# Whitening of two chunks in seven as four 64x64 matmuls at a time, in a float32 whitening, AFNO and MLP kernel

## The chip, the cores and the metric

The kernel runs on one core of one Trainium2 chip. The metric is the device time of one execution in microseconds; lower is better. Engines are named as the profile names them: PE is TensorE (PEld its weight loads), DVE VectorE, ACT ScalarE, POOL GpSimd, SP SyncE.

## The reference

The input is a float32 batch of 16 images of 56x56 pixels with 64 channels. Two layers follow each other.

1. **Whitening.** Over all 50,176 pixels the mean and the 64x64 covariance are taken; with L the Cholesky factor of the covariance (with a little of the unit matrix added), each pixel becomes inverse(L) @ (x - mean), times gamma, plus beta.
2. **An AFNO block.** Layer norm; a real 2D FFT of each image; a small two-layer complex MLP on the spectrum (block diagonal, 8 blocks of 8 channels; relu, then soft shrinkage by 0.01); the inverse FFT, plus its input, plus the residual; a second layer norm; an MLP 64 to 256 to 64 with gelu; plus the residual.

```
f_hat = solve_triangular(cholesky(cov), eye) @ (x - mean);  x1 = f_hat * gamma + beta
h  = afno_filter(layer_norm(x1)) + x1          # rfft2, block MLP, irfft2, + its input
out = gelu(layer_norm(h) @ mw1 + mb1) @ mw2 + mb2 + h
```

## The kernel before

**Tiling.** The 16 images are worked on in 8 pairs. A pair is a tile of 112 partitions (2 images x 56 rows) by 3584 columns (56 pixels x 64 channels), held as 28 blocks of 128 columns; a block has an even pixel column in its first 64 channels and an odd one in its last 64. After a first phase (covariance, elimination, the whitening matrix) the main loop `step(i)`, i = 0 to 7, does the spectral part of pair i, the whitening and first layer norm of pair i+1, the second layer norm and the MLP of pair i-1, and the transposes of pair i+2.

**Whitening.** `transpose_x` (L855) turns the pair's blocks so that the 128 (pixel, channel) rows lie on partitions; ACT copies them to `xT` (L1093). `whiten(i, ks)` (L871) then does chunks of four blocks, seven chunks per pair: for a block, the stationary operand is `xT`'s 128x112 piece, the moving operand is `wy`, 128x128. `wy` holds the 64x64 whitening matrix twice, on its diagonal, and zeros elsewhere. A chunk fills one PSUM bank (112x512). DVE adds beta and writes it to `ybuf` (`ev_whiten`, L623). Pairs from 1 on use bank 0 for chunks 0 to 4 and banks 1 and 2 for chunks 5 and 6. A float32 matmul shows in the trace as two passes, each with a weight load, so a chunk of four matmuls is eight records.

**Order.** Every engine's program is written out by hand, and engines wait for each other by semaphores. In `step(i)` PE does `dft_h(i)` (L887, eight chunks; behind its chunks 2 and 4 come `mlp_out` L982 and `turn_out` L991 of pair i-2's last slice), whitening chunk 0 of pair i+1, `dft_w(i)` (L897), chunk 1, `layer_1(i)` (L910), chunk 2, `transpose_n(i-1, 0)` (L964), chunk 3, and then slices in which the MLP (L973, L982) is mixed with chunks 4 to 6, `layer_2` (L926), `inv_w` (L937) and `inv_h` (L950).

Waits that matter here: `dft_w` begins when ACT has copied all of `dft_h` (L1101). `layer_1` writes the banks of eight chunks; DVE evicts the odd ones, each in two operations (`ev_layer_1`, L632), and ACT the even ones (L1136). `transpose_n(i-1, 0)` begins when all eight are evicted. Chunk k+1 in bank 0 waits until DVE has evicted chunk k, so chunk 3 waits for DVE's eviction of chunk 2.

DVE's program in `step(i)` for i > 1: one eighth of the statistics of pair i-1 (L539), the output add of pair i-2's last slice (`ev_mlp`, L658, waits for L991), the rest of the statistics, `ln2(i-1)` (a chain of small operations, L559 to L415, then the eviction of whitening chunk 0, then two multiplications L582), the eviction of chunk 1, `ev_layer_1(i)`, and the eviction of chunk 2.

**Banks.** Bank 3 (`BANK_M`) belongs to the MLP's transposes and outputs (L964, L982, L991). `c_dve` counts DVE's output adds, seven per pair; `a_dve` counts evicted whitening chunks, seven per pair; `pe_a` counts chunks of transposes and of whitening that PE has finished.

The tile modes of PE that occur: whole array (L855, L871, L887, L897, L937, L964, L991), two parts of 64 rows (L910, L950, L973; L950 has 58 rows and puts the two in banks of their own), and two parts of 64 columns (L926, L982).

Of the kernel before, what the change touches and what calls it, by code (L numbers as in the profile page):

```python
# [25 lines left out]
ALU = mybir.AluOpType  # L26
# [3 lines left out]
B, H, W, C = 16, 56, 56, 64  # L30
# [6 lines left out]
ROWS = 2 * H  # L37
# [16 lines left out]
BANK_X, BANK_M, BANK_HID = 0, 3, 4  # L54
# [31 lines left out]
def before_in_bank(banks):  # L86

    last = {b: k for k, b in enumerate(banks)}
    out = []
    for k, b in enumerate(banks):  # L90
        out.append((last[b], k <= last[b] and b not in banks[:k]))
        last[b] = k
    return out


B_BANK = [(1, 2, 4, 5, 6, 7)[k % 6] if k < L2 else 1 + k % 2 for k in range(B_CHUNKS)]
FIRST_WHITEN = (0, 1, 2, 3, 0, 1, 2)
WHITEN = (BANK_X,) * 5 + (1, 2)
B_BEFORE = before_in_bank(B_BANK)

# [16 lines left out]
C_ACT, C_DVE = len(C_ACT_DONE), SLICES  # L117
# [21 lines left out]
def build(nc, x, consts, params, out):  # L139
# [5 lines left out]
    with ExitStack() as ctx:  # L145
        def sb(name, shape, dtype=F32):
            return ctx.enter_context(nc.sbuf_tensor(name, shape, dtype))

        def sem(name):
            return ctx.enter_context(nc.semaphore(name))  # L150
# [7 lines left out]
        def pp(name, rows=128):  # L158
            return prm[0:rows, p_at[name][0]:p_at[name][1]]

        ident = cc("ident")
        wy = sb("wy", [128, 128])
# [10 lines left out]
        ybuf = sb("ybuf", [ROWS, FREE])  # L173
# [4 lines left out]
        xT = sb("xT", [128, WP * ROWS])  # L178
# [58 lines left out]
        x_in, pe_a, pe_b, pe_c = sem("x_in"), sem("pe_a"), sem("pe_b"), sem("pe_c")  # L237
        a_act, a_dve = sem("a_act"), sem("a_dve")
        b_act, b_dve = sem("b_act"), sem("b_dve")
        c_act, c_dve = sem("c_act"), sem("c_dve")  # L240
# [9 lines left out]
        bank = [psum[:, j, :] for j in range(8)]  # L250
# [20 lines left out]
        def row(name, n):  # L271

            return pp(name, ROWS).unsqueeze(1).broadcast_to((ROWS, n, C))
# [17 lines left out]
        with nc.Block() as block:  # L291
# [116 lines left out]
            def _(dve):  # L408
# [199 lines left out]
                def ln2(i):  # L608
                    mean_rstd(i, 1)
                    if i < PAIRS - 2:  # L610
                        ev_whiten(i + 2, [0])
                    for k in range(2):
                        multiply_rstd(i, k)

                def ev_whiten(i, ks):
                    if i == 1:
                        dve.wait_ge(r_begun, 1)
                    elif i > 1:

                        dve.wait_ge(r_ready, 2 * i - 1)  # L620
                    for k in ks:
                        dve.wait_ge(pe_a, i * A_CHUNKS + 7 + k + 1)
                        nc.vector.tensor_tensor(  # L623
                            ybuf[:, k * 512:(k + 1) * 512].rearrange("p (w c) -> p w c", c=C),
                            bank[(WHITEN if i > 0 else FIRST_WHITEN)[k]][0:ROWS, :].rearrange("p (w c) -> p w c", c=C),
                            row("beta", 8), ALU.add).then_inc(a_dve, 1)
# [54 lines left out]
                def step(i, ahead, behind):  # L681
# [13 lines left out]
                    if behind:  # L695
# [3 lines left out]
                        for k in range(5, 8):  # L699
                            ln2_stats(i - 1, k)  # L700
                        ln2(i - 1)
                    next_(ev_whiten, [1] if behind else [0, 1])
                    ev_layer_1(i)
                    slice_(0, lambda: next_(ev_whiten, [2, 3, 4]), lambda: next_(ev_whiten, [5]),
                           lambda: next_(ev_whiten, [6]), lambda: next_(ln1_stats, [0]))
                    slice_(1, lambda: ev_layer_2(i, [0]), lambda: (ev_layer_2(i, [1]), next_(ln1_stats, [1])),
# [51 lines left out]
            def _(pe):  # L758
# [100 lines left out]
                def whiten(i, ks):  # L859

                    pe.wait_ge(a_act, i * 7 + 7)
                    for k in ks:
                        if i == 0:
                            if k >= 4:
                                pe.wait_ge(a_dve, k - 3)
                        elif 0 < k < 5:
                            pe.wait_ge(a_dve, i * 7 + k)
                        t = bank[(WHITEN if i > 0 else FIRST_WHITEN)[k]]
                        for j in range(4):
                            w = 4 * k + j  # L870
                            last = nc.tensor.matmul(t[0:ROWS, j * 128:(j + 1) * 128], xT[:, w * ROWS:(w + 1) * ROWS],  # L871
                                                    wy[:], start=True, stop=True)
                        last.then_inc(pe_a, 1)
# [135 lines left out]
                def step(i, ahead, ahead2, behind):  # L1009
# [8 lines left out]
                    def whiten_next(j):  # L1018
                        if ahead and j < 3:
                            whiten(i + 1, [4 + j])  # L1020
# [9 lines left out]
                    if ahead:  # L1030
                        whiten(i + 1, [0])
                    dft_w(i)
                    if ahead:
                        whiten(i + 1, [1])
# [326 lines left out]
```

## Time and profile before

| | |
|---|---|
| median of 3 runs | 880.11 us (878.37 to 880.96) |
| profiled execution, its own time | 884.47 us |
| its span, first to last instruction | 882.7 us |
| PE busy | 790.9 us (90%) |
| DVE busy | 577.6 us (65%) |
| ACT busy | 367.1 us (42%) |
| POOL busy | 250.6 us (28%) |
| mean granted TensorE clock | 0.92 of full speed |

A row of the profile names the line, the engine, the operation, what it writes and reads, the shape and the count; times are in microseconds from the start of the span. The PE records of one line that follow each other are merged into one piece with a count of passes. The end of a matmul record is modelled and includes its way through the array, so the time that a group takes from its neighbours is read from start to start. "[0.41 <-X]" is idle time before an instruction and what ended it, as far as the profile can tell; where an instruction waits for several semaphores the name can be the wrong one.

### The profile page before, as it was taken

Reading aid. Unit: us, or ns where it says so; the run is one execution under the profiler, and the core shown is the slowest. Engines: PE = TensorE matmul, PEld = TensorE weight load, DVE = VectorE, ACT = ScalarE, POOL = GpSimd, SP = SyncE. Lnnn points to the kernel's source line nnn. Section 1 sums busy time; section 2 is a strip of 40 time slices with the busy share of each in tenths; the row PEclk is TensorE's granted clock in tenths of the full one; section 3 lists DMA queues with packets and bytes.
Section 4 is the critical chain, followed back from the end, with each engine's and each line's share of the span. In section 5 each row is a group of like instructions: output and inputs, shape, how many; then the busy total and the mean of one; then the engine's idle time right before and its main releaser. Section 6 shows DMA issues by size and latency. Waiting matters only on the chain.

```text
span 882.7 us, 16525 instructions
## 1 busy us (share of the span) xinstructions
PE 790.9 (90%) x6585; PEld 558.3 (63%) x6585; DVE 577.6 (65%) x1868; ACT 367.1 (42%) x660; POOL 250.6 (28%) x106
## 2 busy tenths in 40 slices
PE   5898997598599999999999999999999999899576
PEld 5895655477286658675766767586657755575232
DVE  4465677639666858585876768586858686652621
ACT  0001100263046645564556455545645453555244
POOL 4000000274531271218142604541271228040000
PEclk9996556599789999999999999999999999999889
DMA  9970200200200112011200300130100011001001
GB/s 267 269 184 1 74 0 1 74 0 18 59 1 1 33 32 85 12 33 36 70 23 22 104 2 23 32 95 2 32 27 17 12 33 32 1 22 32 22 28 46
DMA packets 9964, 40.98 MB, mean 46 GB/s; under 512 B 1232, under 2 KB 1232, under 8 KB 8208
## 3 DMA queue, kind: packets, MB, share of 16 engines
q1 hardware_dynamic: 9888, 39.92, 16.1%
q8 instruction: 53, 0.87, 0.4%
q14 instruction: 23, 0.19, 0.1%
HBM read 27.07 MB, written 12.85 MB: 45 GB/s over the span
## 4 chain that ended last, share of the span: by engine, by line
PE 76%; DVE 16%; DMA 4%; issue 3%; ACT 2%; DVEq 0%; ACTq 0%
PE psum L973 11%; PE psum L982 10%; PE psum L887 7%; PE psum L950 6%; PE psum L897 6%; PE psum L926 6%; PE psum L937 6%; PE psum L910 5%; PE psum L871 5%; DMA xin<-x_dram 4%; PE psum L807 3%; PE psum L771 3%; PE psum L855 3%; DVE stats L539 3%; PE psum L991 3%
## 5 line engine op out<-in xcount | busy, mean ns | idle before, releaser
L1156 ACT ACTIVATE hid<-psum,hbias 128x448 f32<-128x448 f32 x224 | 124.1, 635 | 90.7 <-PE psum L973 90.7
L394 POOL TENSOR_TENSOR p_y<-layer,clamped 128x512 f32<-128x512 f32 x64 | 75.4, 1178 | 240.9 <-DVE clamped L649 240.9
L973 PE MATMUL psum<-n2T,mw1s 64*128 64x448 f32 x448 | 104.2, 585 | 3.4 <-ACT n2T L1149 3.4
L982 PE MATMUL psum<-hid,prm 128*64 128x448 f32 x448 | 97.2, 555 | 4.0 <-DVE oslice L658 4.0
L1093 ACT ACTIVATE xT<-psum,negm 128x448 f32<-128x448 f32 x56 | 35.6, 636 | 106.5 <-PE psum L855 106.4
L359 POOL TENSOR_TENSOR hbuf<-hbuf,prm 112x3584 f32<-112x3584 f32 x7 | 43.4, 6200 | 111.0 <-DVE hbuf L604 111.0
L950 PE MATMUL psum<-u_r,cst 58*112 58x448 f32 x256 | 60.4, 592 | 15.5 <-DVE rbuf L671 11.3
L623 DVE TENSOR_TENSOR ybuf<-psum,prm 112x512 f32<-112x512 f32 x56 | 38.6, 689 | 50.7 <-PE psum L871 50.3
L926 PEld LDWEIGHTS psum<-w2s,o_g 128*64 128x64 f32 x1856 | 60.1, 138 | 15.5 <-issue 8.9
L937 PEld LDWEIGHTS psum<-cst,p_y 128*128 128x128 f32 x512 | 61.2, 192 | 11.2 <-issue 5.6
L926 PE MATMUL psum<-w2s,o_g 128*64 128x64 f32 x1856 | 66.3, 224 | 2.1 <-DVE layer L643 2.1
L937 PE MATMUL psum<-cst,p_y 128*128 128x112 f32 x512 | 66.7, 277 | 1.2 <-DVE layer L643 1.2
L982 PEld LDWEIGHTS psum<-hid,prm 128*64 128x64 f32 x448 | 27.4, 137 | 63.7 <-issue 46.7
L643 DVE TENSOR_TENSOR layer<-psum,prm 128x512 f32<-128x512 f32 x64 | 40.4, 631 | 41.5 <-PE psum L926 41.5
L887 PE MATMUL psum<-cst,hbuf 112*112 112x116 f32 x512 | 60.4, 280 | 7.3 <-DVE hbuf L604 5.2
L887 PEld LDWEIGHTS psum<-cst,hbuf 112*112 112x112 f32 x512 | 57.6, 191 | 14.5 <-issue 9.0
L1101 ACT COPY u_r<-psum 112x464 f32<-112x464 f32 x64 | 35.0, 546 | 67.5 <-PE psum L887 67.5
L871 PE MATMUL psum<-wy,xT 128*112 128x128 f32 x448 | 59.5, 282 | 3.8 <-DVE ybuf L623 3.2
L871 PEld LDWEIGHTS psum<-wy,xT 128*112 128x112 f32 x448 | 53.1, 182 | 13.4 <-issue 11.3
L539 DVE BATCH_NORM_STATS2 stats<-ybuf 112x6 f32<-112x64 f32 x448 | 61.2, 209 | 0.5
L973 PEld LDWEIGHTS psum<-n2T,mw1s 64*128 64x128 f32 x448 | 40.5, 193 | 32.1 <-issue 23.8
L897 PE MATMUL psum<-cst,u_r 112*128 112x116 f32 x464 | 53.3, 275 | 0.6 <-ACT u_r L1101 0.6
(116 smaller groups left out, 1310.7 us busy)
## 6 DMA issues: line engine op xcount, KB each, us to landing
xin<-x_dram SPq DMA_DIRECT2D x9, 1568.0 KB, 8.6
out_dram<-oslice SPq DMA_DIRECT2D x56, 224.0 KB, 2.2
ybuf<-x_dram SPq DMA_DIRECT2D x2, 1568.0 KB, 19.3
fbuf<-x_dram SPq DMA_DIRECT2D x2, 1568.0 KB, 22.4
n<-x_dram SPq DMA_DIRECT2D x2, 1568.0 KB, 25.2
xin<-x_dram SPq DMA_DIRECT2D x4, 392.0 KB, 5.1
prm<-params_dram SPq DMA_DIRECT2D x1, 742.0 KB, 26.9
cst<-consts_dram SPq DMA_DIRECT2D x1, 604.0 KB, 18.5
```

Source lines behind the costliest of these rows:

```text
L394: nc.gpsimd.tensor_tensor(yk, a, b, ALU.subtract).then_inc(y_ready, 1)
L539: last = nc.vector.bn_stats(stats[:, w, :], src[:, w * C:(w + 1) * C])
L871: last = nc.tensor.matmul(t[0:ROWS, j * 128:(j + 1) * 128], xT[:, w * ROWS:(w + 1) * ROWS], wy[:], start=True, stop=True)
L887: last = nc.tensor.matmul(t[0:ROWS, j * 2 * KR:(j + 1) * 2 * KR], h_w[:, 4 * k + j, :], cc("f1", ROWS), start=True, stop=True)
L897: last = nc.tensor.matmul(t[:, j * 4 * KF:(j + 1) * 4 * KF], u_r[0:ROWS, (4 * k + j) * 128:(4 * k + j + 1) * 128], cc("f2", ROWS), start=T ...
L910: one = nc.tensor.matmul(t[b][:, 0:(z - a) * KF], w1s[C * b:C * b + C, 256 * s + 128 * half:256 * s + 128 * half + 128], p_v[C * b:C * b + ...
L926: last = nc.tensor.matmul(t[C * r:C * r + C, j * C:j * C + C], o_g[:, at:at + C], w2s[:, 128 * half + C * r:128 * half + C * r + C], start ...
L937: last = nc.tensor.matmul(t[:, j * 112:j * 112 + 112], y_v[:, 4 * k + j, :], cc("invw"), start=True, stop=True)
L950: one = nc.tensor.matmul(t[d][0:ROWS, 0:7 * C], cc("invh")[rows, ROWS * m:ROWS * m + ROWS], g[rows], start=(m == 0), stop=(m == 1))
L973: nc.tensor.matmul(t[:, 0:4 * ROWS], mw1s[C * v:C * v + C, HH * m:HH * m + HH], n2T[C * v:C * v + C, :], start=True, stop=True).then_inc(p ...
L982: last = nc.tensor.matmul(t[C * v:C * v + C, 0:4 * ROWS], pp("mw2")[:, C * m:C * m + C], hid[:, s % 2, m, v, :], start=(m == 0), stop=(m = ...
L1156: nc.scalar.activation(hid[:, s % 2, m, v, :], bank[C_BANK[k]][:, 0:4 * ROWS], ACT.Gelu, bias=hbias[:, m:m + 1]).then_inc(c_act, 1)
```

## The change

For pairs 2 to 7, whitening chunks 0 and 1 are computed in another way. A block of 128x112 by 128x128 becomes four matmuls: stationary 64 rows (even or odd pixel) by 64 or 48 columns (the first 64 and the last 48 image rows of the 112), moving the 64x64 whitening matrix alone. Each of the four has its own quarter of the array. Even pixels go to bank 0 and odd ones to bank 3, 64 columns per block in each, so a chunk fills 256 columns of both banks. DVE evicts each bank with an operation of its own, 112x256, and writes 64-column groups of `ybuf` at a stride of 128; `a_dve` is raised by the second one. A chunk is 16 matmuls (32 passes) in place of 4 (8 passes). Since bank 3 is now written by chunk 0, PE waits ahead of it until DVE has done all the output adds of pair i-2 (of the pair being whitened minus 2), from pair 3 on. Chunks 2 to 6, and pairs 0 and 1, stay as they are.

```diff
+QUADS = (0, 1)
@@ ev_whiten (DVE)
                     for k in ks:
                         dve.wait_ge(pe_a, i * A_CHUNKS + 7 + k + 1)
+                        if i > 1 and k in QUADS:
+                            for v in range(2):
+                                last = nc.vector.tensor_tensor(
+                                    ybuf[:, k * 512:(k + 1) * 512].rearrange("p (w v c) -> p v w c", v=2, c=C)[:, v],
+                                    bank[BANK_M * v][0:ROWS, 0:256].rearrange("p (w c) -> p w c", c=C),
+                                    row("beta", 4), ALU.add)
+                            last.then_inc(a_dve, 1)
+                            continue
@@ whiten (PE)
                         t = bank[(WHITEN if i > 0 else FIRST_WHITEN)[k]]
+                        if i > 1 and k in QUADS:
+                            if k == 0 and i > 2:
+                                pe.wait_ge(c_dve, (i - 2) * C_DVE)
+                            for j in range(4):
+                                for p, m in ((0, C), (C, ROWS - C)):
+                                    for v in range(2):
+                                        at = (4 * k + j) * ROWS + p
+                                        last = nc.tensor.matmul(bank[BANK_M * v][p:p + m, j * C:(j + 1) * C],
+                                                                xT[C * v:C * v + C, at:at + m],
+                                                                wy[C * v:C * v + C, C * v:C * v + C], start=True, stop=True)
+                            last.then_inc(pe_a, 1)
+                            continue
                         for j in range(4):
```

## Rows read from the trace of the kernel before

**Rows 1.** The page: busy time of PE and DVE, granted clock in 40 slices
```profile
PE 790.9 (90%) x6585; PEld 558.3 (63%) x6585; DVE 577.6 (65%) x1868; ACT 367.1 (42%) x660; POOL 250.6 (28%) x106
...
PEclk9996556599789999999999999999999999999889
```

**Rows 2.** Busy time by stretch: two periods of the main loop, and inside one
```profile
core 0: us, PE busy (x) PEld busy (x) DVE busy (x) ACT busy (x) POOL busy (x), PEclk, DMA share, GB/s
...
345.47:428.34 82.87, 81.18 (x736) 56.46 (x738) 60.58 (x195) 45.18 (x81) 29.89 (x12) 1.00 0.14 40
428.34:511.20 82.86, 81.16 (x736) 56.44 (x738) 60.59 (x195) 45.19 (x81) 29.88 (x12) 1.00 0.14 40
```

**Rows 3.** The chain of waits, 420 to 437 us: start, us, what
```profile
420.00 0.88 PE psum L871 x8
...
427.37 0.88 PE psum L871 x8
428.25 5.90 PE psum L910 x32
...
434.17 0.63 DVE o_g L632
...
435.50 0.70 DVE ybuf L623
...
436.33 1.10 PE psum L871 x8
```

**Rows 4.** PE in order of time, the two idle places behind layer_1, second period
```profile
352.70 0.57 PE L964 MATMUL psum<-cst,n 112*128 112x112 f32 x4 [0.41 <-ACT o_g L1136]
353.47 1.10 PE L871 MATMUL psum<-wy,xT 128*112 128x128 f32 x8 [0.19 <-DVE ybuf L623]
```

**Rows 5.** DVE in order of time, 416 to 437 us
```profile
416.87 0.69 DVE L658 TENSOR_TENSOR oslice<-psum,fbuf 112x512 f32<-112x512 f32 x1 [2.06 <-PE psum L991]
417.48 2.75 DVE L539 BATCH_NORM_STATS2 stats<-rbuf 112x6 f32<-112x64 f32 x21
...
424.86 0.69 DVE L623 TENSOR_TENSOR ybuf<-psum,prm 112x512 f32<-112x512 f32 x1
425.47 3.95 DVE L582 TENSOR_TENSOR n<-rbuf,small 112x1792 f32<-112x1792 f32 x2
429.34 0.68 DVE L623 TENSOR_TENSOR ybuf<-psum,prm 112x512 f32<-112x512 f32 x1
430.06 5.41 DVE L632 TENSOR_SCALAR o_g<-psum,prm 64x435 f32<-64x435 f32 x8
435.50 0.69 DVE L623 TENSOR_TENSOR ybuf<-psum,prm 112x512 f32<-112x512 f32 x1
```

**Rows 6.** DVE in order of time, the same place in step(1)
```profile
264.25 5.48 DVE L632 TENSOR_SCALAR o_g<-psum,prm 64x435 f32<-64x435 f32 x8 [0.94 <-PE psum L910]
```

**Rows 7.** The chain of waits, 358 to 368 us: groups in different tile modes
```profile
358.20 0.39 PE psum L964 x4
...
364.28 1.08 PE psum L926 x32
365.37 0.53 PE psum L964 x4
...
367.95 0.73 PE psum L926 x20
```

**Rows 8.** All engines in order of time, around whitening chunk 0
```profile
420.04 0.55 ACT L1101 COPY u_r<-psum 112x464 f32<-112x464 f32 x1 [0.25 <-PE psum L887]
...
420.64 0.30 PEld L897 LDWEIGHTS psum<-cst,u_r 112*128 112x128 f32 x2
420.72 0.29 PE L897 MATMUL psum<-cst,u_r 112*128 112x116 f32 x1
```

**Rows 9.** DVE evictions by shape: count, busy us, mean ns of one
```profile
L643 DVE TENSOR_TENSOR layer<-psum,prm 128x512 f32<-128x512 f32 x48 | 32.7, 681 | 41.5 <-PE psum L926 41.5
...
L643 DVE TENSOR_TENSOR layer<-psum,prm 128x320 f32<-128x320 f32 x16 | 7.7, 480 | 0.0
```

## The prediction

> **What bounds the kernel now.** I read the page first, for the engines' shares and the clock, then the busy time of two whole periods, then the chain of waits through one period, and then each engine in order of time around the two chunks that change.
>
> PE is busy for 790.9 us of the 882.7 us span, DVE for 577.6 us; the granted clock is below full speed only in the first part, which the change doesn't touch [rows 1]. A period of the loop is 82.87 us, PE is busy for 81.2 us of it, and the clock is 1.00 throughout (2.4 GHz) [rows 2]. By these shares PE is the bound, and any PE time saved would be time saved. The chain says otherwise for one place: it runs through chunk 0 (0.88 us), chunk 1 (0.88) and layer_1 (5.90), then leaves PE for DVE at 434.17, goes through DVE's last layer_1 eviction (L632) and its eviction of whitening chunk 2 (L623), and returns to PE with chunk 3 at 436.33 [rows 3]. PE stands still there twice, 0.41 us ahead of L964 and 0.19 us ahead of chunk 3 [rows 4]. The row gives ACT as what ended the first; but DVE's last L632 ends at 430.06 + 5.41 = 435.47, and the same wait asks for it, so DVE is as likely.
>
> How free DVE is to follow PE decides what the change is worth. From 416.87, when L991 releases it, DVE shows no idle time for a PE result until 436.19: an output add, statistics, the small chain, chunk 0's eviction at 424.86, two multiplications, chunk 1's at 429.34, eight layer_1 operations from 430.06, chunk 2's at 435.50 [rows 5]. What starts that run of DVE work, L991 inside dft_h, lies ahead of both changed chunks. So PE and DVE reach 434.17 together: the chain may be drawn through PE, but DVE alone would come to the same moment. In step(1) it isn't so: DVE waited 0.94 us for layer_1 and then took 5.48 us in place of 5.41 [rows 6].
>
> **PE's part.** A whitening pass of 128 columns takes 0.88 / 8 = 110 ns [rows 3], so a 64-column pass alone should take some 55 ns. Where two parts of the array work side by side on 64 columns (L926), 32 passes take 1.08 us and 20 take 0.73 [rows 7]: (1.08 - 0.73) / 12 = 29 ns a pass, or 58 ns for two at once, and 1.08 - 32 x 0.029 = 0.15 us that doesn't depend on the count. The same 0.15 us shows on the other side: a whole-array group of 4 takes 0.53 us between two column-tiled groups and 0.39 us among its own kind [rows 7]. I take 0.15 us as the price of one change of tile mode.
>
> No row shows four parts at once. Bounds: four at a time at the pass's own length, 8 x 55 ns = 0.44 us for the 32 passes; two at a time, 32 x 29 ns = 0.93 us; one at a time, 32 x 55 ns = 1.76 us. I take four at a time, each round a little longer than the 58 ns of two, 0.48 us: L926 shows two parts overlapping nearly fully in columns, and L910 does in rows (32 passes of 435 or 406 columns, at 110 / 128 ns a column, would be some 11.6 us in a line and take 5.90 [rows 3]). The change puts the two row halves in different banks, as L910 does.
>
> Chunk 0 stands between dft_h and dft_w, both whole-array: two mode changes, 0.48 + 0.30 = 0.78 us against 0.88. But dft_w waits for ACT's last copy of dft_h, which ends at 420.04 + 0.55 = 420.59; dft_w's first weight load starts at 420.64, its first pass at 420.72 [rows 8]. The chunk was just long enough to cover ACT, so the 0.10 us is worth nothing: PE waits instead. Chunk 1 stands ahead of layer_1, which changes the mode anyway: one more change, 0.48 + 0.15 = 0.63 us against 0.88. Layer_1 starts and ends 0.25 us earlier. The new wait for `c_dve` costs nothing: the add that it wants is done at 416.87 + 0.69 = 417.56 [rows 5], over 2 us before chunk 0 at 420.00; behind it on PE stands everything else, but it would bind only if DVE came 2.4 us later. The later users of bank 3 already wait for DVE work that stands behind chunk 1's eviction. No DMA is touched or moved.
>
> **DVE's part.** An eviction of 512 columns becomes two of 256. In L643, 192 columns more take 681 - 480 = 201 ns [rows 9], 1.05 ns a column, so 256 columns last about 0.69 - 0.27 = 0.42 us. One operation starts before the last has fully ended: L582 starts 425.47 - 424.86 = 0.61 us after the 0.69 us eviction starts [rows 5], an overlap of 0.08. Two take 2 x (0.42 - 0.08) = 0.68 us where one took 0.61: 0.07 us more. From the statistics the fixed part is a little less: 21 operations of 64 columns in 2.75 us [rows 5] are 0.13 us each, 0.067 of it columns, 0.06 fixed. The bounds are 0.06 and, with no overlap at all, 0.84 - 0.61 = 0.23; I take 0.075 a chunk, 0.15 us a pair. Half the columns in each of two banks saves nothing.
>
> **The sum.** In steps 2 to 6, DVE's run from 416.87 is unbroken, so its last L632 ends 0.15 us later, and L964 and chunk 3 with it. PE's 0.25 us goes into its own wait. From there on PE is the bound again and everything moves by the same amount. That is 5 x 0.15 = +0.75 us. In step(1) DVE follows PE: -0.25 us (it has 0.94 us of idle time to lose, and 5.41 us is still shorter than its present 5.48). Together +0.5 us: span 883.2, that execution's own time 884.97. The profiled execution, 884.47, stands 4.4 us above the median of 880.11, and the change goes onto the median: **880.6 us**. About 0.3% (2.6 us) is what a measurement of this kernel can tell from no change; this forecast is within it.
>
> **Rivals.**
>
> *A. Two at a time.* The 29 ns a pass of L926 may be what the engine can start, not what two parts can do. Each chunk streams 0.93 us: chunk 0 takes 0.93 + 0.30 = 1.23 (+0.35, and ACT no longer covers it), chunk 1 takes 0.93 + 0.15 = 1.08 (+0.20). Layer_1 ends 0.55 us later, DVE follows PE, and its own 0.15 is covered: 6 x 0.55 = +3.3 us, **883.4**. This is the case on the slower side; it decides once a chunk streams for over 0.73 us, since two chunks then cost PE 2 x 0.73 + 0.45 - 1.76 = 0.16 us, more than DVE's 0.15. Between the forecast and this, three quarters of the way at 0.82 us a chunk, PE would lose 2 x 0.82 - 1.31 = 0.33 us a pair, +2.0 us. For it: no row shows passes closer than 29 ns on average. Against: 29 ns is just half of a pass plus a little, as two parts would give, and layer_1 overlaps as fully at some 370 ns for two passes (5.90 / 16), where starting can't be the limit. The Trainium skill, "TensorE: Matmul & The Clock Gate", section "Wait — 56ns, not 53.3ns?", has a floor of its own: matmuls never start less than about 25 ns apart, however short. By that estimate the chunk streams 32 x 25 = 0.80 us, costs PE +0.22 and +0.07, and the whole comes to +1.7 us; no row here is short enough to show it.
>
> *B. One at a time.* If the four parts get in each other's way (two banks and two column halves at once), 1.76 us a chunk: +1.18 and +1.03 us, 6 x 2.2 = +13 us, **893**. Only that nothing of the kind stands in the trace speaks for it.
>
> *C. PE's gain goes through.* If ACT's and DVE's rows hide slack, all of 0.10 + 0.25 us a pair counts: -2.1 us, **878.0**, still within 0.3%. To be faster by more, mode changes would have to be free as well: 12 x 0.40 = -4.8 us. Against both: DVE's unbroken run.
>
> *D. The change does not do what it says*, and the quarters run as whole-array matmuls: 32 passes of 55 ns without mode changes, much as B.
>
> **How the numbers follow.** Forecast (DVE decides, PE's gain lost) 0.55; the case between it and A, +2.0 us, 0.15; A 0.15; B and D 0.06; C 0.09. The range takes in the forecast, C, the case in between and most of A: 878.6 to 883.6. A median of three moves by about 1 us either way. Slower by over 0.3% (above 882.75): B and D, nearly all of A, a little of the case in between, 0.23. Faster (below 877.5): a part of C, 0.04. Within: 0.73.
>
> **What the changed profile would show.** Right: L871 chunks of 32 passes at 0.5 to 0.8 us; dft_w still starting 0.68 us after the last L1101 does, with PE idle ahead of it; two L623 of about 0.42 us per chunk; the idle time ahead of L964 grown from 0.41 to some 0.8 us in steps 2 to 6, with DVE as its end; a period of 83.0 us. Wrong: 32 passes at 1.1 us or more, and DVE waiting ahead of L632 in every step (A, B); a period below 82.87 (C). It would fail altogether if the pieces outside the two chunks changed length.

## The result, and the profile after

The changed kernel was timed three times against the kernel before. The first timing, 20 executions each, gave a median of 881.84 us (877.89 to 887.47) against 878.13 (874.79 to 890.68), ratio 1.0045 with an interval of 1.0026 to 1.0064. The two later ones, among the experiments below, gave 0.9992 (0.9962 to 1.0023) and 0.9967 (0.9941 to 0.9993). The first and the third contradict each other, so the timings as a whole don't show a sign. The traces can be compared more closely: the loop below repeats to 0.03 us between two executions of the kernel before and to 0.10 us between three of the changed kernel.

First the loop as a whole. PE in order of time, the start of each `dft_w`, changed kernel:

```profile
251.45 6.73 PE L918 MATMUL psum<-cst,u_r 112*128 112x116 f32 x58
334.06 6.73 PE L918 MATMUL psum<-cst,u_r 112*128 112x116 f32 x58
417.06 6.73 PE L918 MATMUL psum<-cst,u_r 112*128 112x116 f32 x58
...
583.06 6.73 PE L918 MATMUL psum<-cst,u_r 112*128 112x116 f32 x58
666.44 6.73 PE L918 MATMUL psum<-cst,u_r 112*128 112x116 f32 x58
748.13 6.73 PE L918 MATMUL psum<-cst,u_r 112*128 112x116 f32 x58 [0.64 <-ACT u_r L1122]
```

and the same three ends in the kernel before:

```profile
254.98 6.66 PE L897 MATMUL psum<-cst,u_r 112*128 112x116 f32 x58
337.85 6.66 PE L897 MATMUL psum<-cst,u_r 112*128 112x116 f32 x58
...
750.80 6.73 PE L897 MATMUL psum<-cst,u_r 112*128 112x116 f32 x58 [0.63 <-ACT u_r L1101]
```

The six stretches from dft_w(1) to dft_w(7), each holding one changed chunk 1 and one changed chunk 0, take 748.13 - 251.45 = 496.68 us; before it was 750.80 - 254.98 = 495.82. The change costs **0.86 us** there, 0.10% of the whole. 0.07 us of it is only a matter of where the reading starts: wherever a changed chunk 0 stands ahead of it, `dft_w` lasts 6.73 us in place of 6.66, and so it does in both kernels at dft_w(7), which has no chunk ahead; from the end of dft_w(1) to the end of dft_w(7) the loss is 0.79. Step by step: 82.61 us in step 1 (before 82.87), 83.00 in steps 2 to 4, 83.38 in step 5, 81.69 in the last (before 81.48).

Step 7, which has no whitening, differs too. PE in order of time behind layer_1(7), the kernel before, then the changed kernel:

```profile
764.86 0.58 PE L964 MATMUL psum<-cst,n 112*128 112x112 f32 x4 [1.47 <-ACT o_g L1136]
766.05 3.43 PE L973 MATMUL psum<-n2T,mw1s 64*128 64x448 f32 x8 [0.62 <-ACT n2T L1149]
769.41 0.61 PE L964 MATMUL psum<-cst,n 112*128 112x112 f32 x4
```

```profile
762.19 0.57 PE L985 MATMUL psum<-cst,n 112*128 112x112 f32 x4 [1.47 <-ACT o_g L1157]
763.39 1.84 PE L994 MATMUL psum<-n2T,mw1s 64*128 64x448 f32 x8 [0.62 <-ACT n2T L1170]
765.16 0.60 PE L985 MATMUL psum<-cst,n 112*128 112x112 f32 x4
```

The same eight passes take 3.43 us and 1.84 us: behind the same idle places of 1.47 and 0.62 us the mean granted clock is 0.71 in the kernel before (764.80 to 767.80 us; it fell from 2.4 to 1.2 GHz there) and 1.00 in the changed kernel (762.13 to 765.13). From dft_w(7) to the last pair's transposes (L964, in the changed kernel L985) it is 78.64 us before and 77.36 after, 1.28 less. That outweighs the loss in the loop: from dft_w(1) to that point the kernel before takes 574.5 us (`null` 574.3) and the changed kernel 574.1 (its second and third profile 573.9), and from dft_w(1) to the end of the span 627.7 us against 627.3, 625.8 and 625.7. So the traces show a loop that is longer by 0.8 to 0.9 us, and from dft_w(1) on a kernel that isn't longer. What follows explains the loop; why the clock stays up in step 7 is open.

Where the loop's loss goes: all engines in order of time, step 2 of the changed kernel (POOL, DVE and PE lines; the rows answer to [rows 4, 5, 8]).

```profile
330.28 0.69 DVE L667 TENSOR_TENSOR oslice<-psum,rbuf 112x512 f32<-112x512 f32 x1 [2.07 <-PE psum L1012]
330.89 2.75 DVE L540 BATCH_NORM_STATS2 stats<-fbuf 112x6 f32<-112x64 f32 x21
331.05 4.05 POOL L385 TENSOR_TENSOR rbuf<-hbuf,ybuf 112x1792 f32<-112x1792 f32 x1 [4.20 <-DVE oslice L667]
...
333.35 0.68 PE L885 MATMUL psum<-wy,xT 64*64 64x64 f32 x32
333.46 0.55 ACT L1122 COPY u_r<-psum 112x464 f32<-112x464 f32 x1 [0.25 <-PE psum L908]
333.68 1.54 DVE L560 TENSOR_TENSOR small<-stats 112x56 f32<-112x56 f32 x1
334.05 6.55 PEld L918 LDWEIGHTS psum<-cst,u_r 112*128 112x128 f32 x58 [0.16 <-ACT u_r L1122]
...
338.29 0.76 DVE L626 TENSOR_TENSOR ybuf<-psum,prm 112x256 f32<-112x256 f32 x2
338.96 3.95 DVE L583 TENSOR_TENSOR n<-fbuf,small 112x1792 f32<-112x1792 f32 x2
340.72 0.68 PE L885 MATMUL psum<-wy,xT 64*64 64x64 f32 x32
341.33 5.92 PE L931 MATMUL psum<-p_y,w1s 64*128 64x435 f32 x32
342.82 0.75 DVE L626 TENSOR_TENSOR ybuf<-psum,prm 112x256 f32<-112x256 f32 x2
343.61 5.41 DVE L641 TENSOR_SCALAR o_g<-psum,prm 64x435 f32<-64x435 f32 x8
...
349.12 0.58 PE L985 MATMUL psum<-cst,n 112*128 112x112 f32 x4 [0.81 <-ACT o_g L1157]
```

Chunk 1 takes 341.33 - 340.72 = 0.61 us from start to start against 0.97 in the kernel before by the same reading (427.21 to 428.18). Not all of these 0.36 us are a gain, since some 0.1 us now stands ahead of the chunk: in `pool_chunk1`, where only chunk 1 is changed, it is 7.20 us from the start of dft_w to that of layer_1, before 7.46 (420.72 to 428.18), 0.26 less. Behind chunk 0 the weight load of dft_w waits for ACT. DVE's evictions take 0.67 and 0.79 us to the next instruction, before 0.61 and 0.72. The wait ahead of L985 is 0.81 us, before 0.41; the row names ACT, but DVE's last L641 ends at 343.61 + 5.41 = 349.02, just ahead of it, and `dve_split` below, where only DVE's work is longer, lengthens the same wait. One row stands out: DVE's L560, a small operation of 56 columns, lasts 1.54 us. POOL's L385 ends at 331.05 + 4.05 = 335.10, L560 at 335.22.

### The profile page after: what moved, and what is told of

Read it like the earlier page. It is cut to its first block, busy times and chain, and to the rows that moved or that the text cites. A ratio compares the mean times of both kernels' runs of the same rounds, so it can differ in the third digit from the quotient of the medians.

```text
span 878.7 us, 17118 instructions
## 1 busy us (share of the span) xinstructions
PE 785.2 (89%) x6873; PEld 551.9 (63%) x6873; DVE 578.8 (66%) x1880; ACT 367.1 (42%) x660; POOL 250.9 (29%) x106
## 4 chain that ended last, share of the span: by engine, by line
PE 65%; DVE 25%; DMA 4%; issue 4%; ACT 2%; DVEq 0%; ACTq 0%
PE psum L994 11%; PE psum L1003 10%; PE psum L971 7%; PE psum L947 6%; PE psum L958 6%; PE psum L908 5%; DVE stats L540 4%; DMA xin<-x_dram 4%; PE psum L892 4%; DVE o_g L641 3%; PE psum L816 3%; PE psum L780 3%; PE psum L864 3%; PE psum L1012 3%; PE psum L918 2%
## 5 line engine op out<-in xcount | busy, mean ns | idle before, releaser
L908 PE MATMUL psum<-cst,hbuf 112*112 112x116 f32 x512 | 57.9, 272 | 7.3 <-DVE hbuf L605 5.2
L908 PEld LDWEIGHTS psum<-cst,hbuf 112*112 112x112 f32 x512 | 55.1, 184 | 14.5 <-issue 9.0
L1122 ACT COPY u_r<-psum 112x464 f32<-112x464 f32 x64 | 35.0, 546 | 65.0 <-PE psum L908 65.0
L632 DVE TENSOR_TENSOR ybuf<-psum,prm 112x512 f32<-112x512 f32 x44 | 30.4, 690 | 46.8 <-PE psum L892 46.6
L918 PEld LDWEIGHTS psum<-cst,u_r 112*128 112x128 f32 x464 | 52.4, 192 | 1.8 <-ACT u_r L1122 1.8
L369 POOL TENSOR_TENSOR rbuf<-ybuf,prm 112x3584 f32<-112x3584 f32 x1 | 7.8, 7757 | 158.9 <-DVE hbuf L605 158.9
```

The source lines that it names most:

```text
L908: last = nc.tensor.matmul(t[0:ROWS, j * 2 * KR:(j + 1) * 2 * KR], h_w[:, 4 * k + j, :], cc("f1", ROWS), start=True, stop=True)
L918: last = nc.tensor.matmul(t[:, j * 4 * KF:(j + 1) * 4 * KF], u_r[0:ROWS, (4 * k + j) * 128:(4 * k + j + 1) * 128], cc("f2", ROWS), start=T ...
```

## The experiments

The loop is compared by the same six stretches throughout, dft_w(1) to dft_w(7), in us:

```
kernel        step 1  step 2  step 3  step 4  step 5  step 6    sum
before         82.87   82.87   82.86   82.87   82.87   81.48   495.82
null           82.87   82.87   82.87   82.88   82.87   81.49   495.85
changed        82.61   83.00   83.00   83.00   83.38   81.69   496.68
dve_split      82.87   82.98   83.01   82.99   83.37   81.60   496.82
chunk1         82.60   82.92   82.94   82.90   82.94   81.55   495.85
one_evict      82.61   82.85   82.92   82.84   82.85   81.54   495.61
stats_after    82.61   82.96   83.05   82.97   83.36   81.67   496.62
pool_before    82.87   82.87   82.87   82.86   82.88   81.49   495.84
pool_after     82.61   82.61   82.61   82.61   82.96   81.31   494.71
pool_chunk1    82.61   82.61   82.61   82.61   82.61   81.24   494.29
shift10        82.87   82.87   82.88   82.88   83.22   81.50   496.22
```

**null: the kernel before against itself.** No edit.

> The kernel before against itself. Both theories: ratio 1.000, an interval of some +-0.3%, a period of 82.87 us in its profile. It shows how far two sets of executions of one program stand apart, and whether the first 250 us (where the clock is below full speed) differ from one execution to the next by as much as the 4 us between the two profiles at hand.

Ratio 1.0003 (0.9985 to 1.0022). The loop is the same to 0.03 us, and yet this profile's span is 878.8 us against 882.7. The stretch ahead of the loop differs: PE in order of time, `null` first, then the kernel before.

```profile
241.35 1.76 PE L950 MATMUL psum<-u_r,cst 58*112 58x448 f32 x8 [1.30 <-DVE rbuf L671]
243.88 6.57 PE L887 MATMUL psum<-cst,hbuf 112*112 112x116 f32 x64 [0.77 <-DVE rbuf L671]
```

```profile
240.79 3.33 PE L950 MATMUL psum<-u_r,cst 58*112 58x448 f32 x8 [1.30 <-DVE rbuf L671]
244.89 9.38 PE L887 MATMUL psum<-cst,hbuf 112*112 112x116 f32 x64 [0.77 <-DVE rbuf L671]
```

The busy time by stretch gives a granted clock of 1.00 between 245 and 255 us for `null` and 0.72 for the kernel before: the clock rose from its lower level (1.2 GHz) to the full one (2.4 GHz) after PE's idle places of step 0, in one execution in time for dft_h(1), in the other in the middle of it. From dft_w(0) to dft_w(1) the profiles show three lengths, about 70.4, 71.9 and 74.7 us, in kernels of either kind. That one stretch spreads by over 4 us, five times the loss in the loop; the stretch ahead of it, up to dft_w(0), takes 175.0 to 182.1 us.

**again and again2: the changed kernel, second and third time.** No edit.

> The changed kernel, a second profile. Theory 1 (DVE's two evictions set the loss and the rest is chance): period 83.01 us in every step from 2 on, sum over the loop +0.5 to +1.0 us against the kernel before, ratio 1.0006 to 1.0012 but for chance. Theory 2 (something in the changed kernel adds about 3 us more, such as stalls that come now and then, or a clock that falls more often): periods of 83.3 us or more in several steps, or a lower granted clock in the loop, ratio 1.003 or more again.

> The changed kernel a third time. The first timing gave a ratio of 1.0045 (1.0026 to 1.0064), the second 0.9992 (0.9962 to 1.0023), while the loop, in both profiles, is 0.8 us longer (0.1%). If the loop's 0.8 us is all, the ratio is near 1.001 again and the first timing was chance in the first and last stages; if not, near 1.004.

Ratios 0.9992 and 0.9967, as above; the loops sum to 496.60 and 496.58 us, periods 82.61, 82.98, 83.0, 82.98, 83.35, 81.7. So the loop's 0.8 us is a property of the program, and the first timing's 3.7 us isn't in the loop. Theory 2 in its form of 3 us more in the loop falls; the one stall in step 5 stands. Why three timings of the same two programs disagree beyond their intervals was not found; the stretches whose clock differs from run to run are the candidates, and only the profiled executions show those. Step 7's isn't one of them. Its MLP ran at the lower clock in all five profiles of kernels that evict each chunk whole (`before`, `null`, `pool_before`, `shift10`, `one_evict`) and at full clock in all nine of the others. So it went with the program; but it isn't PE's part of the change (`dve_split` keeps the clock, `one_evict` doesn't) nor the number of DVE instructions (`shift10`), and no run isolates what it is.

**dve_split: only DVE's part of the change.**

```diff
+                        if i > 1 and k < 2:
+                            for v in range(2):
+                                last = nc.vector.tensor_tensor(
+                                    ybuf[:, k * 512:(k + 1) * 512].rearrange("p (w v c) -> p v w c", v=2, c=C)[:, v],
+                                    bank[BANK_X][0:ROWS, :].rearrange("p (w v c) -> p v w c", v=2, c=C)[:, v],
+                                    row("beta", 4), ALU.add)
+                            last.then_inc(a_dve, 1)
+                            continue
```

> The kernel before, PE untouched; only the evictions of whitening chunks 0 and 1 of pairs 2 to 7 are two operations of 256 columns each instead of one of 512. Theory 1: the period goes from 82.87 to 83.0 us in steps 2 to 6 with no change on PE, the idle time ahead of L964 from 0.41 to 0.55, total +0.7 to +0.9 us, ratio 1.001. Theory 2 (PE's quarter matmuls cost the time): period 82.87, ratio 1.000.

The periods are those of the changed kernel in steps 2 to 5, with PE as before. PE in order of time, step 3:

```profile
422.63 5.92 PE L918 MATMUL psum<-p_y,w1s 64*128 64x435 f32 x32
428.48 1.13 PE L879 MATMUL psum<-wy,xT 128*112 128x128 f32 x8
430.16 0.57 PE L972 MATMUL psum<-cst,n 112*128 112x112 f32 x4 [0.55 <-ACT o_g L1144]
```

The wait grew from 0.41 to 0.55 us: DVE's fixed cost alone makes the loss, and from step 2 on the quarter matmuls neither add to it nor take from it. The sum is +1.00 us, more than was expected, by the long step 5. Ratio 0.9991 (0.9963 to 1.002).

**stats_after: DVE relieved of 1.8 us ahead of its chain.** In the changed kernel:

```diff
-                        ln2_stats(i - 1, 4)
+                        for k in (4, 5, 6):
+                            ln2_stats(i - 1, k)
                         if i > 1:
                             ev_mlp(i - 2, SLICES - 1)
-                        for k in range(5, 8):
-                            ln2_stats(i - 1, k)
+                        ln2_stats(i - 1, 7)
```

> The changed kernel, with two of DVE's eighths of the second layer norm's statistics (14 operations, 1.8 us) moved ahead of the output add that waits for L991, into 2.06 us in which DVE stood idle. Theory 1: DVE is now ahead, PE's shorter chunk 1 counts, the period is 82.87 - 0.25 = 82.6 us in every step from 1 on, the idle time ahead of L964 is back at 0.4, total -1.5 us against the kernel before, ratio 0.998. Rival (PE's gain is lost to something else, or the quarter matmuls cost elsewhere): the period stays at 82.87 or more.

Theory 1 failed here: the periods stayed at 83.0 us, and the ratio is 1.0008 (0.998 to 1.0035). POOL and DVE in order of time, step 3:

```profile
417.73 0.98 DVE L540 BATCH_NORM_STATS2 stats<-rbuf 112x6 f32<-112x64 f32 x7
417.89 4.08 POOL L385 TENSOR_TENSOR fbuf<-hbuf,ybuf 112x1792 f32<-112x1792 f32 x1 [4.17 <-DVE oslice L667]
418.74 3.35 DVE L560 TENSOR_TENSOR small<-stats 112x56 f32<-112x56 f32 x1
```

L560 started 1.8 us earlier and lasted 1.8 us longer. It ends at 422.09, POOL's operation at 421.97: the same 0.12 us behind it as in the changed kernel. Elsewhere in these traces the same operation lasts about 0.26 us. DVE's operation waits for POOL's, inside its own record. Both read two SBUF operands. The Trainium skill, "SBUF — State Buffer", section "SBUF: two separate sides", says that VectorE and GpSimd share one pair of SBUF ports as an exclusive lock, held for a whole instruction, and that a VectorE operation with two SBUF inputs takes it against a GpSimd operation that reads SBUF; the trace agrees (statistics, with one input, run beside POOL at their usual pace in the rows above, and so does an output add in the kernel before, a TENSOR_TENSOR with one input in SBUF and one in PSUM: it lasts 0.68 us from 411.45, in the middle of a POOL add of 409.43 to 413.46). The lock itself is on no row; that POOL's end sets DVE's is what the next runs test. Theory 1b: the start of DVE's chain is set by POOL's add, which waits for L667, which waits for L1012 of PE.

**pool_before and pool_after: POOL's add split, so that little of it is left when L667 is done.** In each of the two kernels:

```diff
-                    for k in range(2):
-                        ws = slice(k * WP, (k + 1) * WP)
+                    for lo, hi, s in ((0, 28, 3), (28, 48, 5), (48, 56, 6)):
+                        ws = slice(lo, hi)
                         if i > 1:
-                            pool.wait_ge(c_dve, (i - 2) * C_DVE + out_done(3 + 3 * k))
-                        nc.gpsimd.tensor_tensor(r4[i % 2][:, ws], h_tok[:, ws], y4[:, ws], ALU.add).then_inc(r_ready, 1)
+                            pool.wait_ge(c_dve, (i - 2) * C_DVE + out_done(s))
+                        last = nc.gpsimd.tensor_tensor(r4[i % 2][:, ws], h_tok[:, ws], y4[:, ws], ALU.add)
+                        if s != 5:
+                            last.then_inc(r_ready, 1)
```

> The kernel before; POOL's second residual add is split so that only its last 8 of 28 pixel columns wait for DVE's last output add (L658), 1.15 us of work after it in place of 4.04. In all traces so far DVE's first small operation of the second layer norm ended 0.12 us after this POOL operation did, however early it started (1.54 us long, 3.35 us in stats_after, 0.26 elsewhere). Theory 1b (POOL's add, not DVE's own work, sets when DVE's chain begins): that operation shrinks to 0.27 us, the chain runs 1.27 us earlier, but PE bounds layer_1, so the period stays at 82.8 to 82.87 us. Rival (DVE's own work was the bound): the operation and the period stay as they are.

> The same POOL split in the changed kernel. Theory 1b: DVE is 1.1 us ahead of layer_1, its longer evictions are covered, PE's shorter chunk 1 counts, and the period is 82.6 us in every step from 1 on, total -1.5 us against the kernel before (ratio 0.998). Rival (PE's gain has nowhere to go whatever DVE does): 82.87 or more.

DVE and POOL in order of time in `pool_after`, step 3:

```profile
411.80 2.75 DVE L542 BATCH_NORM_STATS2 stats<-rbuf 112x6 f32<-112x64 f32 x21
411.96 1.29 POOL L385 TENSOR_TENSOR fbuf<-hbuf,ybuf 112x512 f32<-112x512 f32 x1 [1.29 <-DVE oslice L669]
414.59 0.27 DVE L562 TENSOR_TENSOR small<-stats 112x56 f32<-112x56 f32 x1
...
422.46 0.75 DVE L628 TENSOR_TENSOR ybuf<-psum,prm 112x256 f32<-112x256 f32 x2
424.04 5.48 DVE L643 TENSOR_SCALAR o_g<-psum,prm 64x435 f32<-64x435 f32 x8 [0.83 <-PE psum L933]
```

The small operation is back at 0.27 us, DVE waits 0.83 us for layer_1, and the period is 82.61 us: the 0.26 us of chunk 1 now counts in every step. In the kernel before the same edit is worth nothing (495.84): DVE is early there too (0.94 us idle ahead of its layer_1 evictions), but PE arrives when it did. The periods are as expected but for step 5 of `pool_after`, 82.96 us, which makes its sum -1.1 us where -1.5 was expected. Ratios 1.0007 (0.9977 to 1.0036) for `pool_after` and 1.0006 (0.9973 to 1.0039) for `pool_before`: too wide to see 1.1 us.

**chunk1, pool_chunk1 and pool_chunk1b: quarter matmuls for chunk 1 alone.** `QUADS = (1,)`, with the wait for `c_dve` moved to chunk 1; the last two with POOL's add split.

> The changed kernel with quarter matmuls for chunk 1 only, POOL as before. One eviction is split instead of two: DVE, released by POOL's add, ends layer_1's evictions 0.07 us later than in the kernel before, so the period is 82.94 us in steps 2 to 6 and 82.61 in step 1, total +0.1 us. Rival (the loss comes from chunk 0's part on PE): 82.87.

> As pool_after, but only chunk 1 is done by quarter matmuls; chunk 0 is whole-array as before. Theory (chunk 0's shortening is worth nothing, since dft_w waits for ACT's last copy of dft_h): period 82.6 us, the same as pool_after. Rival (both chunks count): some 0.1 us more than pool_after.

> pool_chunk1 a second time, with more rounds: periods of 82.61 us in steps 1 to 6 as in its first profile, 1.5 us less than the kernel before in sum, ratio 0.998; whether a timing can tell that from 1.000 is open, since its interval has been +-0.3%.

`chunk1` has 82.92 us in step 2, half of the changed kernel's loss. `pool_chunk1` has 82.61, the same as `pool_after`: chunk 0's shorter time is worth nothing. Both its profiles sum to 494.29 us in the loop, 1.53 less than the kernel before. PE in order of time, the second profile:

```profile
327.97 6.65 PE L920 MATMUL psum<-cst,u_r 112*128 112x116 f32 x58
410.58 6.66 PE L920 MATMUL psum<-cst,u_r 112*128 112x116 f32 x58
```

Ratios: 0.9981 (0.9943 to 1.0019) for `chunk1`; 0.9989 (0.9959 to 1.0018) and 0.9957 (0.9929 to 0.9985), 877.12 us against 879.57, for `pool_chunk1`. It has the shortest loop of all; the loop accounts for 0.9983, all from dft_w(1) to the end for 0.9976 (625.6 and 625.7 us against 627.7), and the rest of 0.9957 is no more explained than the first timing's 1.0045.

**one_evict: quarter matmuls, but one DVE operation per chunk.** Banks 1 and 3 change places so that the two halves lie side by side:

```diff
-                            for v in range(2):
-                                last = nc.vector.tensor_tensor(
...
-                            last.then_inc(a_dve, 1)
+                            both = psum[0:ROWS, 0:2, 0:256]
+                            nc.vector.tensor_tensor(
+                                ybuf[:, k * 512:(k + 1) * 512].rearrange("p (w v c) -> p v w c", v=2, c=C),
+                                both.rearrange("p v (w c) -> p v w c", c=C),
+                                pp("beta", ROWS).unsqueeze(1).unsqueeze(1).broadcast_to((ROWS, 2, 4, C)),
+                                ALU.add).then_inc(a_dve, 1)
```

The banks change places in `bank = [psum[:, (0, 3, 2, 1, 4, 5, 6, 7)[j], :] for j in range(8)]`.

> The changed kernel with PE's quarter matmuls as they are, but DVE evicts a chunk with one operation that reads 256 columns of each of two banks side by side (banks 1 and 3 are swapped for that). Theory 1 (the second eviction's fixed cost is the loss): period back to 82.87 us in steps 2 to 6, 82.6 in step 1, total -0.25 us against before. It also has as many DVE instructions as the kernel before: if the 0.35 us that three kernels with a longer DVE program lost ahead of inv_h's eviction in step 5 came from where the program's instructions lie, it is gone. Rival (a read over two banks costs as much as two operations): period 83.0.

One operation over two banks lasts 0.69 us, as over one:

```profile
424.50 0.69 DVE L626 TENSOR_TENSOR ybuf<-psum,prm 112x512 f32<-112x512 f32 x1
```

Periods of 82.85 us in three of the steps 2 to 5, 82.92 in the other, sum -0.21 us against before, as expected within 0.05; why one step is 0.07 longer isn't known. The stall of step 5 is gone too. Ratio 0.9995 (0.9962 to 1.0029).

**shift10: ten unused DVE operations early in the kernel before.**

```diff
+                    for n in range(10):
+                        nc.vector.tensor_copy(pad[:, n * C:n * C + C], ident[0:C, 0:C])
                     link(nc.vector.tensor_copy(elim[:, 1, C:2 * C], ident[0:C, 0:C]))
```

> The kernel before with ten more small DVE operations (64x64 copies into a tile that nobody reads) in the covariance phase, so that every later DVE instruction lies ten places further on in its program, as it does in the changed kernel by step 5; nothing in the loop is altered. If the 0.35 us that DVE lost in step 5 ahead of inv_h's eviction comes from where the instructions lie, the step-5 period is 83.2 us or the stall shows at another place in the loop, and all other periods are 82.87. If it comes from the work that DVE does in the loop, all periods are 82.87.

In the one execution that was taken, step 5 takes 83.22 us and steps 1 to 4 82.87 or 82.88. The stall is at the same instruction. DVE in order of time, step 5: the changed kernel, `shift10`, and `null`.

```profile
640.22 2.02 DVE L605 TENSOR_TENSOR hbuf<-hbuf,small 112x1792 f32<-112x1792 f32 x1
645.96 1.16 DVE L680 TENSOR_TENSOR fbuf<-psum,fbuf 112x448 f32<-112x448 f32 x2 [3.72 <-PE psum L971]
```

```profile
640.13 2.02 DVE L607 TENSOR_TENSOR hbuf<-hbuf,small 112x1792 f32<-112x1792 f32 x1
645.87 1.16 DVE L674 TENSOR_TENSOR fbuf<-psum,fbuf 112x448 f32<-112x448 f32 x2 [3.72 <-PE psum L953]
```

```profile
639.58 2.02 DVE L604 TENSOR_TENSOR hbuf<-hbuf,small 112x1792 f32<-112x1792 f32 x1
644.97 1.16 DVE L671 TENSOR_TENSOR fbuf<-psum,fbuf 112x448 f32<-112x448 f32 x2 [3.37 <-PE psum L950]
```

The idle time ahead of the inv_h eviction is 3.72 us in the first two and 3.37 in the last. PE isn't late, though the rows name it: in the changed kernel its last pass ends 0.11 us ahead of DVE's start in step 4 and 0.46 us ahead in step 5. By step 5 the changed kernel has ten DVE instructions more than the kernel before; ten that do nothing bring the same 0.35 us. `chunk1`, with five more, doesn't have it, nor does `one_evict`, with none.

## Why the prediction was right, and where it was not

**PE's part** held. Four parts do run at once: the 32 passes of a chunk start in eight groups of four, mostly some 56 ns from group to group, and rivals A, B and D are out. Step 1, where DVE follows PE, gained 0.26 us, forecast 0.25, so chunk 1 costs 0.88 - 0.26 = 0.62 us, forecast 0.63. The floor that rival A cites from the Trainium skill, "TensorE: Matmul & The Clock Gate", section "Wait — 56ns, not 53.3ns?", about 25 ns from start to start and by that estimate 0.80 us a chunk, did not hold across the four parts: 0.61 us for 32 passes, 19 ns each.

**Chunk 0 worth nothing** held: dft_w's weight load waits for ACT in the row above, and `pool_chunk1` is as fast without the quarter matmuls of chunk 0.

**DVE's part** held in size: two evictions cost 0.06 and 0.07 us more (forecast 0.075 each), `dve_split` alone lengthens the period of steps 2 to 4 by 0.11 to 0.15 us, and `chunk1` by about half of it. L985's wait is 0.81 us, forecast 0.8, and the period 83.00, forecast 83.0.

**What set DVE's chain** was named wrongly. The prediction took DVE to be unbroken at work from 416.87, with L991 as its release. L991 is at the head, but between it and the chain stands POOL's add of 4.05 us, and 1.27 us of the "work" was a 56-column operation that waited for POOL. The period came out right by luck, because a chain that starts at POOL's end is as rigid as one of work; a remedy drawn from the prediction (`stats_after`: give DVE less to do) did nothing. The row was there to be read: the small operation lasts six times its sisters, and its end follows a POOL record's end.

**The sum** was +0.5 us; the loop shows +0.86, 0.79 without the 0.07 us of reading. Steps 2 to 4 gave 0.13 to 0.14 each and the last one 0.21 - 0.07 = 0.14, against 0.15; the difference is the 0.35 us of step 5, which was on no row of the kernel before. The sum also left out step 7. The prediction took the granted clock to be below full speed "only in the first part"; the page's own row ends in 8, 8, 9 [rows 1], and in step 7 the clock fell as well. That fall is gone in the changed kernel, -1.28 us, and with it the sum up to the last pair's transposes is -0.4 us, not +0.5. By the prediction's own sign, pieces outside the two chunks changed length, in steps 5 and 7: the mechanism at the two chunks is right, the account of the whole kernel isn't complete. (A slip without effect: 2 x 0.73 + 0.45 - 1.76 is 0.15, not 0.16.)

**The forecast of the time**, 880.6 us and no measurable difference, stands against 881.84 in the first timing, within the range. That timing by itself called the change 0.45% slower, outside the 0.3% that the forecast allowed; the two later ones do not repeat it, and the loop accounts for 0.10%. That 881.84 is near 880.6 is in part luck as well: the forecast stands on a median of 880.11 us from three runs, and the 20 runs beside the first timing had 878.13, so that timing showed +3.7 us where +0.5 was forecast. Rival C's condition, DVE with slack, was made true in `pool_after`, and PE's gain then went through, at 0.26 us a step rather than 0.35, since chunk 0's share has no use. The idle place ahead of dft_w was as forecast in kind, but its first pass starts 0.60 us after the last L1122 does, not 0.68 (334.06 - 333.46).

## What to carry to other kernels

A shorter stage pays only where the next engine is waiting for it: follow the chain one engine further than the profile draws it, and ask what started that engine's run. An operation that lasts several times what its sisters of the same shape last is a wait, even with no idle time shown; look for the record of another engine that ends just before it. Where the effect sought is a tenth of a per cent, compare the periods of the loop in the traces, then the stretches behind the loop too, since a gain or a loss of the clock there can be larger than the effect, and leave the whole time to larger effects.

## What the runs showed that was not expected

- A DVE addition with two SBUF inputs waited inside its own record for a POOL addition to end: 1.54 us in place of 0.26, and 3.35 us when it was started 1.8 us earlier, ending 0.12 us behind POOL each time.
- Ten more instructions in DVE's program, ahead of the loop or in it, cost 0.35 us at one later instruction, the same one in each case. What lies behind it was not tested.
- The granted clock fell in step 7 in all five profiles of kernels that evict a chunk with one operation and in none of the nine others, a matter of 1.1 to 1.3 us. What decides it is open.
- One DVE operation that reads 256 columns of each of two neighbouring PSUM banks took as long (0.69 us) as one that reads 512 of one bank.
- 32 float32 passes of 64x64 parts ran in 0.61 us, 19 ns a pass where two parts at a time had never shown less than 29 [rows 7].
- One execution differs from the next by up to 4.4 us in the 70 to 75 us after dft_w(0), with the moment at which the granted clock rises.
